# A banded-kernel attention and mixture-of-experts layer: the second half of the attention stage in a new order, its column sums moved from ScalarE to VectorE, and both ends of the stage rearranged

## What is computed

```
q, k, v = heads(layernorm(x) @ w_qkv.T + b_qkv);  q, k = l2norm(q), l2norm(k)
cos   = clip(q @ k.T, -1 + 1e-7, 1 - 1e-7)
score = (1 + arccos(cos)) ** (-3.2)
n_r   = sum over keys of score;  n_c = sum over queries of score
probs = score / n_r / n_c, each row divided by its sum
x     = x + (probs @ v) @ w_out.T + b_out
u     = layernorm(x);  s = softmax(u @ centroids.T + expert_biases)
out   = x + u + sum over the 2 best of 16 experts of s_e * (u @ Wr_e.T + br_e)
          + mean of 2 shared experts of (u @ Ws.T + bs)
```

## Time and profile before

| | |
|---|---|
| median of 3 runs | 5292.97 us |
| profiled execution, its own time | 5294.67 us |
| its span, first to last instruction | 5293.0 us |
| ScalarE (ACT) busy | 4881.8 us, 92% |
| VectorE (DVE) busy | 3768.9 us, 71% |
| TensorE (PE) busy | 3117.3 us, 59% |
| GpSimd (POOL) busy | 1808.3 us, 34% |
| mean granted TensorE clock | 0.72 of 2.4 GHz |

### The profile page before, as it was taken

One profiled execution on the slowest core, in us unless ns is written; L12 is line 12 of the kernel. 1 busy time (PEld: TensorE's weight loads), 2 busy tenths in 40 slices (PEclk: granted clock), 3 DMA queues, 4 the chain that ended last, 5 costly groups with the idle time before them and its releaser, 6 DMA issues. The chain is left out here.

```text
span 5293.0 us, 37761 instructions
## 1 busy us (share of the span) xinstructions
PE 3117.3 (59%) x10544; PEld 803.4 (15%) x10678; DVE 3768.9 (71%) x3925; ACT 4881.8 (92%) x1711; POOL 1808.3 (34%) x545
## 2 busy tenths in 40 slices
PE   8645555555555455555456646565655566565699
PEld 4200000111110000000001111111111111111244
DVE  7767777778787777777667576666867576666466
ACT  5799999999999999999989999999999999999421
POOL 0224433344433444333432444334432444334000
PEclk9856586666766766776656777686777768786799
DMA  2100000000000000000000101010100101010200
GB/s 88 64 8 14 18 18 12 13 18 18 18 14 18 10 10 10 10 9 3 12 29 26 34 18 44 10 44 10 42 20 26 34 18 44 10 44 2 84 31 13
DMA packets 71847, 128.17 MB, mean 24 GB/s; under 512 B 9654, under 2 KB 46937, under 8 KB 71706
## 3 DMA queue, kind: packets, MB, share of 16 engines
q1 hardware_dynamic: 70554, 122.50, 7.3%
q0 software_dynamic: 1152, 4.19, 0.3%
HBM read 96.77 MB, written 29.88 MB: 24 GB/s over the span
## 5 line engine op out<-in xcount | busy, mean ns | idle before, releaser
L1120 POOL TENSOR_TENSOR X<-X 128x2048 f32<-128x2048 f32 x504 | 1799.9, 3608 | 2958.7 <-DVE X L929 2958.7
L800 PE MATMUL psum<-stacks 128*128 128x512 bf16 x3962 | 1710.7, 525 | 1028.3 <-DVE X L943 628.9
L943 DVE TENSOR_TENSOR X<-psum,X 128x1024 f32<-128x1024 f32 x1024 | 1194.9, 1218 | 690.0 <-ACT X L1152 678.7
L929 DVE TENSOR_SCALAR X<-psum 128x1024 f32<-128x1024 f32 x1024 | 1186.4, 1216 | 18.9 <-PE psum L800 14.7
L825 PE MATMUL psum<-X,vp 128*32 128x512 f32 x4096 | 628.0, 774 | 780.4 <-DVE vp L959 780.3
L1152 ACT ACTIVATE X<-X 128x4096 f32<-128x4096 f32 x256 | 904.8, 3605 | 0.7
L1144 ACT ACTIVATE X<-X,consts 128x8192 f32<-128x8192 f32 x128 | 903.8, 7108 | 0.0
L1160 ACT ACTIVATE X<-X 128x4096 f32<-128x4096 f32 (+1 forms) x192 | 897.8, 4739 | 2.6 <-DVE X L943 2.5
L1168 ACT ACTIVATE X<-X,consts 128x16384 f32<-128x16384 f32 x64 | 892.9, 13951 | 0.8
L951 DVE TENSOR_REDUCE ncol<-X 128x4 f32<-128x8192 f32 x64 | 555.8, 8684 | 296.2 <-ACT X L1173 296.2
L800 PEld LDWEIGHTS psum<-stacks 128*128 128x128 bf16 x4096 | 259.2, 105 | 2482.6 <-DVE X L943 1441.6
(11 more groups left out here) (167 smaller groups left out, 1439.7 us busy)
## 6 DMA issues: line engine op xcount, KB each, us to landing
V<-expert_w SPq DMA_DIRECT2D x64, 512.0 KB, 3.6
stacks<-qk_parts SPq DMA_DIRECT2D x256, 64.0 KB
qk_parts<-X SPq DMA_DIRECT2D x96, 128.0 KB, 1.9
stacks<-qk_parts SPq DMA_DIRECT2D x64, 192.0 KB
head_out<-evac SPq DMA_DIRECT2D x32, 256.0 KB, 2.1
expert_w<-u_t SPq DMA_DIRECT2D x17, 256.0 KB, 2.6
X<-in_L_attn_x_dram POOLq DMA_DIRECT2D x8, 512.0 KB, 4.2
stacks<-qk_parts SPq DMA_DIRECT2D x32, 128.0 KB
```

The costliest lines, as they stand in the source:

```text
L800: return nc.tensor.matmul(dst, stacks[:, 1, buf, keys:keys + P], stacks[:, 0, buf, q0:q0 + n], start=True, stop=True)
L929: nc.vector.tensor_scalar(X[:, m % 2, i, j * CW:(j + 1) * CW], ps_cos[j % 2], -CLIP, CLIP, ALU.max, ALU.min).then_inc(cos_ok, 1)
L943: nc.vector.tensor_tensor(part, ps_cos[j % 2], part, ALU.mult).then_inc(cos_ok, 1)
L1120: nc.gpsimd.tensor_tensor(own, own, own, ALU.mult).then_inc(square_ok, 1)
```

## The change

In the second half of the stage VectorE takes all column sums, and ScalarE's exponential is the two-piece one of the first half. The order of the side work changes too: VectorE does mults, then the small side work of the block, then the clips with one half-chunk's gather after each clip tile; TensorE follows with the same order, the first clip tile ahead of the side work. The first block of side work (k = 8, m = 0) keeps its place. In the last block (n = 63) chunks 4 to 8 stand ahead of values and adds instead of behind them.

At the start of the stage, SyncE's last 12 stores of `qk_parts` move from the first stage into the second, and VectorE waits for them only between the clips of block 0 and those of block 1, which overwrite the stored buffer.

```diff
@@ SyncE, end of the first stage and start of the second
                 for h in range(2):
                     load_stacks(sp, 0, h)
-                for m in range(2):
-                    step(TURNS - 1, m)
-                for m in range(2):
-                    sp.wait_ge(parts_out[m], TURNS * 192 + 1)
+                store_parts(sp, TURNS - 1, 0)
...
+                store_parts(sp, TURNS - 1, 1)
+                for m in range(2):
+                    sp.wait_ge(parts_out[m], TURNS * 192 + 1)
                 periods(sp, emit)
@@ TensorE
                 def emit(k, m, beside):
+                    todo = halves(m) if beside == "tail" else []
+                    if ends(k, m):
+                        side_work(k, m)
+                        for c, h in todo:
+                            side_chunk(k, c, h)
+                        todo = []
...
                     if has(k, m + 2):
-                        for i in range(BT):
+                        clip(k, m + 2, 0)
+                    if beside == "tail" and not starts(k, m) and not ends(k, m):
+                        side_work(k, m)
+                    for i in range(BT):
+                        if i and has(k, m + 2):
                             clip(k, m + 2, i)
+                        for c, h in todo[i:i + 1]:
+                            side_chunk(k, c, h)
+                    for c, h in todo[BT:]:
+                        side_chunk(k, c, h)
...
-                    if beside == "tail":
+                    if starts(k, m):
                         side_work(k, m)
-                        side_chunks(k, *CHUNKS.get(m, (0, 0)))
@@ VectorE
-                        values(k, m, piece, beside != "tail")
+                        values(k, m, piece)
...
-                    if has(k, m + 2):
-                        for i in range(BT):
+                    if beside == "tail" and not starts(k, m):
+                        if m == 0:
+                            steps[0] = SCALE_STEPS + (k - SIDE) * PAIR_STEPS
+                        side_work(k, m)
+                    for i in range(BT):
+                        if has(k, m + 2):
                             clip(k, m + 2, i)
+                        for c, h in todo[i:i + 1]:
+                            side_gather(k, c, h)
+                    for c, h in todo[BT:]:
+                        side_gather(k, c, h)
...
-                for n in range(2):
-                    for i in range(BT):
-                        clip(0, n, i)
+                for i in range(BT):
+                    clip(0, 0, i)
+
+                for m in range(2):
+                    dve.wait_ge(parts_out[m], TURNS * 192 + 1)
+                for i in range(BT):
+                    clip(0, 1, i)
@@ ScalarE
-                        if beside != "tail":
-                            own = tiles(m, a, b)
-                            nc.scalar.activation(own, own, ACT.Exp, scale=POWER).then_inc(score_ok, 1)
-                            continue
-
-                        act.wait_ge(vp_ok, n * len(EXP_PIECES))
-                        for i in range(a, b):
-                            own = X[:, m % 2, i, :]
-                            last = nc.scalar.activation(own, own, ACT.Exp, scale=POWER, accum_out=ncol[:, i:i + 1])
-                        last.then_inc(score_ok, 1)
+                        own = tiles(m, a, b)
+                        nc.scalar.activation(own, own, ACT.Exp, scale=POWER).then_inc(score_ok, 1)
```

More of the change, by code:

```diff
@@ L613, in pre_ln_arccos_attention_moe_kernel, with halves @@
         CHUNKS = {2: (0, 4), 3: (4, NC)}
+        def halves(m):
+            return [(c, h) for c in range(*CHUNKS.get(m, (0, 0))) for h in range(2)]
         en_in = sem("en_in")
@@ L688, in has, with starts, ends @@
             return not (isinstance(k, int) and 4 * k + m >= NB)
+        def starts(k, m):
+            return isinstance(k, int) and k == SIDE and m == 0
+        def ends(k, m):
+            return isinstance(k, int) and 4 * k + m == NB - 1
         with nc.Block() as block:
@@ L745, in side_after @@
                     if m == 3:
[L746 to L751, removed]
+                        for c in range(3):
+                            side_chunk(k + 1, c)
+                        side_store(k)
                 def emit(k, m, beside):
@@ L787, in emit @@
                         sp.dma_start(dst, e_t).then_inc(et_out, 16)
[L788 removed]
+                    if beside == "tail" and not ends(k, m):
                         side_after(k, m)
+                store_parts(sp, TURNS - 1, 1)
+                for m in range(2):
+                    sp.wait_ge(parts_out[m], TURNS * 192 + 1)
                 periods(sp, emit)
@@ L829, in add, with side_chunk @@
                     mm.then_inc(sum_ps, 1)
-                def side_chunks(k, a, b):
-                    for c in range(a, b):
+                def side_chunk(k, c, h):
+                    if h == 0:
                         pe.wait_ge(side_w[c % 3], ((k - SIDE) * 3 + c // 3 + 1) * 16)
[L835 to L845, removed]
+                    wide = D if c == NC - 1 else 2 * D
+                    wait(pe, side_e_ok, (k - SIDE) * 2 * NE + (4 * c + 2 * h - 2 if c else h - 1))
+                    dst = ps_side[h][:, 0:wide]
+                    for kc in range(KC):
+                        mm = nc.tensor.matmul(dst, u2_t[:, h, kc, :], w_ring[c % 3][:, kc, 0:wide],
+                                              start=(kc == 0), stop=(kc == KC - 1 and wide == 2 * D))
+                    if wide == D:
+                        mm = nc.tensor.matmul(dst, gate2_t[:, h, :], be_rows[:, :], start=False, stop=True)
+                    mm.then_inc(side_e_ps, 1)
                 def side_work(k, m):
@@ L943, in mult, with values @@
                         nc.vector.tensor_tensor(part, ps_cos[j % 2], part, ALU.mult).then_inc(cos_ok, 1)
-                def values(k, m, piece, own):
+                def values(k, m, piece):
                     n = 4 * k + m
```

77 lines of the change are left out of this document (37 added, 40 removed).

## The result

The changed kernel took 5258.77 us (median of 4 runs, 5258.32 to 5259.19), against 5291.68 for the kernel before on the same chip (5290.24 to 5293.99): a ratio of 0.9937, 95% interval 0.9925 to 0.9949. Forecast was 5250 with a range of 5236 to 5278. So the sign and the range held, and 32.9 us were gained of 42.9.

What follows compares the result with a forecast made beforehand. ScalarE was taken to set the pace, with VectorE's lateness the second question. Terms -39.0 - 5.8 - 2.5 + 7.0 + 2.7 - 9.3 + 4.0 = -42.9 us took 5294.67 to 5251.8, forecast as 5250, range 5236 to 5278.

Steps and rivals of the forecast that it cites:

- exponentials, 30 blocks: ScalarE's second-half exponentials: 15.16 us shrink to 13.86, 1.30 us a block in 30 of 32 blocks, 39.0 us gained.
- logits waits: ScalarE's eight waits for the side work's first logits step disappear, as logits stand some 20 us earlier: 5.8 us gained.
- old arctangent waits: The 2.5 us that ScalarE's arctangents wait in the kernel before are replaced by the new waits.
- new waits at the places of blocks 2 and 3: Mixed clips and half-chunks make VectorE late behind blocks 2 and 3 of seven pairs: 7.0 us lost.
- first pair: Side chain keeps its place and its 18.6 us wait; values behind it now need reductions: 2.7 us lost.
- beginning: Start of the attention stage: with 12 stores behind the barrier, TensorE starts at 192.7, 9.3 us earlier.
- end: End of the attention stage: block 63's gathers, then both reductions, adds and evacuation finish 4.0 us later than before.
- I take 0.5 us of waiting at each of the 14 places: Blocks 2 and 3 of seven pairs: estimated margins 0.3 and 0.9 us, so 7.0 us of waiting in all.
- The slack of 4.2 us: How late VectorE's values may come in a second-half block before ScalarE waits for mult tiles: 4.2 us.
- margins: Slack left behind blocks 2 and 3, 0.3 and 0.9 us, called no margins at all with such estimates.
- Sums too late: Rival: PSUM handovers stretch mixed tiles to 3.75 us, 14 places lose 3 us more each: 5292, no change; chance 0.13.
- Half clock: Rival: TensorE stays at half clock in mixed tiles and becomes the bound: 5425, or about 5331 if half slow; chance 0.08.

Runs made afterwards that it cites:

- the run with the wait put off: Changed kernel, VectorE waiting for a half-chunk's second gather only ahead of the next gather into the same rows, two tiles later: 5238.18 us.
- the run with the turned loop: Changed kernel, VectorE's loop over pairs jumping back ahead of block 1's mults instead of behind block 3, same order of work: 5254.36 us.
- two small edits: Changed kernel with the wait behind a gather put off and the last block's column sums accumulated by ScalarE again: 5222.09 us.
- the old order with the sums: Kernel before, with VectorE's column sums in the second half too, side work and borders as they were: 5446.49 us.

## Why the prediction was right, and which term was mis-sized

The prediction named the right bound and the right mechanism, and most terms came out close:

| term | forecast, us | measured, us |
|---|---|---|
| exponentials, 30 blocks | -39.0 | -41.7 |
| logits waits | -5.8 | -5.8 |
| old arctangent waits | -2.5 | -2.6 |
| new waits at the places of blocks 2 and 3 | +7.0 | +21.1 |
| first pair | +2.7 | +1.1 |
| beginning | -9.3 | -9.9 |
| end | +4.0 | +4.0 |

The exponentials are read from ScalarE's long logarithms: a block without waits is 74.05 long before and 72.66 after, 1.39 less rather than 1.30, thirty times. The column sums to -33.8 of the span's -35.5; the rest is spread over the stages.

**The step that was mis-sized** is "I take 0.5 us of waiting at each of the 14 places". It was 11 places: six behind block 2 with 0.81 to 2.27, together 9.5, and five behind block 3 with 2.23 to 2.48, together 11.6. The first pair's two places and the last one behind block 3 had no wait. The slack of 4.2 us in that step was nearly right: reductions that begin 12.9 after the exponentials are 5.8 later than the 7.06 of an undelayed block, so 1.6 of waiting was due, and the six waits average 1.6; behind block 3 they begin 14.5 after them on average, 7.4 late, so 3.2 were due and 2.3 came. What was wrong was the lateness. Forecast were 3.9 behind block 2 and 3.3 behind block 3; measured were 5.8 and 7.4. The first difference, 1.9, is the tile: seven of them at 3.57 us, not 3.3, that is the 0.30 behind each gather in the loop. The row of the gather's length doesn't hold it, since the last pair is written out and nothing followed the gathers there but other gathers; the run with the wait put off shows it. The second, 4.1, is the same 1.9 and the jump back, 3.35 to 5.02, which the run with the turned loop shows, less some 1.8 by which the forecast had the first tile of block 3 too late: it put its end at 57.5, where its own terms (51.8 + 0.6 + 3.3) give 55.7.

Where no loop is in the way, the forecast came out nearly as reckoned. In the first pair, with tiles of 3.30 and no jump, the reductions behind block 2 begin 10.91 us after their exponentials (2847.51 - 2836.60), so 3.9 late as forecast; those behind block 3 begin 8.66 after (2917.92 - 2909.26), 1.6 late, where 55.7 would give 1.5; and neither place has a wait:

```profile
2836.60 13.96 ACT L1208 ACTIVATE X<-X 128x8192 f32<-128x8192 f32 x2
...
2847.51 8.69 DVE L978 TENSOR_REDUCE ncol<-X 128x4 f32<-128x8192 f32 x1
...
2909.26 13.95 ACT L1208 ACTIVATE X<-X 128x8192 f32<-128x8192 f32 x2
...
2917.92 8.67 DVE L978 TENSOR_REDUCE ncol<-X 128x4 f32<-128x8192 f32 x1
```

So the step failed in taking the gather's length in a written-out pair for its cost in the loop, and in putting the jump back at nothing. The gap at the jump could have been seen: the timeline of VectorE in the kernel before has it at the same jump, in idle time that cost nothing there:

```profile
3539.59 0.18 DVE L957 RECIPROCAL vp<-ncol 128x4 f32<-128x4 f32 x1 [3.90 <-DVEq L953]
```

The prediction said of its margins that with such estimates they aren't margins; it then priced them nearly as if they were. That the end came out at +4.0 is in part luck: the last values were written 1.4 us sooner after the last logarithm than reckoned (at 4932.41, 49.2 behind it for 50.6), and adds and evacuation took 6.15 for 4.5:

```profile
4937.87 0.69 DVE L1119 COPY evac<-psum 128x512 f32<-128x512 f32 x1 [5.46 <-PE psum L841]
```

The six waits behind block 2 differ because TensorE's adds ahead of the second mult tile differ: where these take 6.4 to 6.5 us, the wait is 2.05 to 2.27, where they take about 5.2, it is 0.81 to 1.15. The length of the adds goes with TensorE's granted clock around them: 0.55 to 0.59 in the 7 us around each of the three long ones, 0.72 to 0.76 in the 6 or 7 us around the others.

**The gap at the jump.** The page "Runtime: NRT & Kernel Launch" of the Trainium skill (section Instruction fetch mechanics) says that a taken branch whose target isn't held makes the engine wait for a DMA fetch. The trace agrees, with 3.35 to 5.02 us at each of the five jumps, nothing at entry or exit, and one packet of the instruction queue in each of the five gaps. In the run with the turned loop such packets stand behind VectorE's jump at its new place (3301.2), where no other engine jumps. That nothing but the fetch makes up the gap is not shown.

**The wait of 0.30.** The Trainium skill (VectorE: DVE Perf Modes, section The DRAIN you can't avoid) says that eight copies took as long with a semaphore after each as with one after the last only. The written-out first pair comes close to that, with 0.03 us between a gather and the clip that waits for it. In the loop the wait keeps the register instructions behind it from running beside the gather, and that is what the 0.30 and the put-off wait show.

**The rivals.** Sums too late: its mechanism is what happened, with VectorE's own wait in place of PSUM handovers, at a third of its price (some 14 us more than forecast at those places, where it had 42). Half clock: refuted, the granted clock of the mixed tiles is 1.00, where the clips alone had 0.50. So the swing that the Trainium skill warns of (TensorE: Matmul & The Clock Gate, section A second HAM failure mode: psum-queue depth-cycling) isn't seen in these tiles either, though TensorE waits in every one. The side work ahead of the clips runs at the short lengths, 0.19 us, as was assumed; in the old order the same instruction takes 3.30 beside GpSimd (L1035 above). The first cosine begins at 192.37 (forecast 192.7), and VectorE's clips of blocks 0 and 1 follow each other without a gap (193.04 to 229.69), so it doesn't wait for the moved stores:

```profile
3110.08 0.19 DVE L1060 TENSOR_TENSOR small<-small 128x32 f32<-128x32 f32 x1
...
192.37 1.49 PE L816 MATMUL psum<-stacks 128*128 128x512 bf16 x3 [4.68 <-DMA stacks<-qk_parts]
```

## What to carry to other kernels

When work is moved onto an engine that has little slack, count its loop as part of its time: the jump back, and the register instructions that come to stand behind a wait on its own result. Idle time hid both in the kernel before, and they came to light when that was spent. A length read from a written-out stretch need not hold in a loop. An order that makes room and the work that is put into it are two gains of their own, so each is worth a run by itself: here the order and the borders without the work gave nearly all that the whole change gave, and two small edits then made the work worth 40.5 us. At the border of a stage the other engine can be the better place for the same work: the sums of the last block belong to ScalarE, which has nothing else to do there.

## What the runs showed of the hardware that was not expected

- A clip that waits for the gather right ahead of it starts 0.30 us behind it in a loop, where register instructions of 69 and 99 ns follow the wait, and 0.03 in the written-out pair, where none do. With the wait put off by two tiles they run beside the gather.
- VectorE's jump back to the start of its long loop leaves it idle for 3.35 to 5.02 us, with one packet of the instruction queue in each gap; entry and exit do not.
- Products and sums of small SBUF operands (two numbers or 32) take 0.19 us where GpSimd is idle and up to 3.5 where it squares, but the reductions among them (0.19 in the old order with the sums) and the gathers of 256 columns (0.99 for two) keep their length beside it.
- In the third stage one turn in 16 was some 3.5 us longer in one program than in others that compute the same in it; why is open.
